# Expert dispatch sent by batch of eight token tiles instead of all at once, in a fused cross-attention and mixture-of-experts kernel

## The reference

```python
def ffn(x):                                # x: 4096 x 256, after _layernorm
    s = softmax(x @ gate_w.T); orig = s; s = s + gate_b
    # the sum of the best two in each of 4 groups picks 2 groups, then the best 2 experts of those
    idx, weights = top2(within_best_two_groups(s), values=orig)
    combine = (one_hot(idx, 16) * weights[..., None]).sum(1)
    h = silu(einsum('td,edi->tei', x, We1) + be1) * (einsum('td,edi->tei', x, We3) + be3)
    yo = einsum('tei,eid->ted', h, We2) + be2
    y = einsum('te,ted->td', combine, yo)
    z = silu(x @ ws1 + bs1) * (x @ ws3 + bs3) @ ws2 + bs2
    return y + z

x = x + align(ctx, _layernorm(x))          # dynamic time warping, its path, a scatter-add of ctx rows
x = x + ffn(_layernorm(x))
```

## Time and profile before

| | us |
|---|---|
| median of 3 runs | 546.51 (544.09 to 548.3) |
| the profiled execution's own time | 549.24 |
| its span, first to last instruction | 547.5 |
| mean granted TensorE clock | 0.806 |
| busy: PE, DVE, ACT, POOL | 309.6, 368.4, 180.0, 162.1 |
| busy share: PE, DVE, ACT, POOL | 57%, 67%, 33%, 30% |

### The profile page before, as it was taken

One profiled execution on the slowest core, in us unless ns is written; L12 is line 12 of the kernel. 1 busy time (PEld: TensorE's weight loads), 2 busy tenths in 40 slices (PEclk: granted clock), 3 DMA queues, 4 the chain that ended last, 5 costly groups with the idle time before them and its releaser, 6 DMA issues.

```text
span 547.5 us, 10073 instructions
## 1 busy us (share of the span) xinstructions
PE 309.6 (57%) x2103; PEld 220.7 (40%) x2105; DVE 368.4 (67%) x2023; ACT 180.0 (33%) x457; POOL 162.1 (30%) x186
## 2 busy tenths in 40 slices
PE   5820000000005879849883796688999998999100
PEld 4720000000002654324441562577888887878000
DVE  4869999999993696896830521635655565555297
ACT  3662000000000155651360624344665555555000
POOL 8000000000000032100777476424555555555200
PEclk9975555555556799988998799788999999999755
DMA  8305989999703000000552132133444443433499
GB/s 330 139 16 157 311 219 236 221 231 226 245 1 89 0 2 0 1 0 1 155 202 106 49 107 87 67 99 121 143 147 142 142 132 100 148 121 94 176 389 355
DMA packets 54961, 75.37 MB, mean 138 GB/s; under 512 B 11206, under 2 KB 45324, under 8 KB 53263
## 3 DMA queue, kind: packets, MB, share of 16 engines
q1 hardware_dynamic: 47983, 58.15, 37.1%
q0 software_dynamic: 6912, 16.83, 8.6%
q10 hardware_dynamic: 32, 0.02, 0.0%
HBM read 39.42 MB, written 37.64 MB: 141 GB/s over the span
## 4 chain that ended last, share of the span: by engine, by line
DVE 41%; PE 33%; another core or an unknown queue 6%; issue 6%; DMA 5%; ACT 5%; POOL 1%; DVEq 1%; SPq 0%; ACTq 0%; POOLq 0%
PE psT L854 14%; PE psT L864 6%; DVE xk L1286 5%; DVE V L1050 3%; DVE R L1018 3%; PE psD L844 3%; DVE A L1056 3%; DVE M L1024 3%; PE psT L801 2%; DVE F L1016 2%; DVE mask L1046 2%; DVE M L1014 2%; DVE A L1057 2%; PE psT L752 2%
## 5 line engine op out<-in xcount | busy, mean ns | idle before, releaser
L482 POOL DMA_INDIRECT results<-ys,idx x80 | 78.9, 986 | 79.1 <-issue 44.9
L854 PE MATMUL psT<-xsT,w_now 128*128 128x128 f32 x640 | 91.3, 287 | 6.4 <-issue 2.1
L683 PE MATMUL psT<-onesb 128*128 128x512 bf16 x24 | 9.1, 557 | 136.5 <-DVE mask L1046 136.5
L854 PEld LDWEIGHTS psT<-xsT,w_now 128*128 128x128 f32 x640 | 79.9, 196 | 15.5 <-issue 12.5
L474 POOL DMA_INDIRECT slot_rows<-stage,slot x64 | 62.8, 981 | 67.9 <-DVE slot L1208 36.1
L465 POOL TENSOR_SCALAR x2n<-xk,sm 128x256 f32<-128x256 f32 x16 | 9.0, 569 | 200.3 <-DVE sm L1082 192.9
L801 PE MATMUL psT<-x2T,sw 128*128 128x512 f32 x128 | 59.9, 618 | 12.8 <-DVE silu L1100 11.5
L683 PEld LDWEIGHTS psT<-onesb 128*128 128x128 bf16 x24 | 3.2, 136 | 141.8 <-issue 141.5
L1274 DVE SCALAR_TENSOR_TENSOR hgT<-psT,w,sg 128x128 f32<-128x128 f32 x80 | 28.1, 351 | 45.7 <-ACT sg L643 30.1
L864 PE MATMUL psT<-w,hgT 128*128 x160 | 49.8, 393 | 3.4 <-DVE hgT L1274 3.4
L634 ACT ACTIVATE w_now<-w 128x256 f32 x80 | 33.3, 417 | 44.5 <-PE psD L844 35.9
(11 more groups left out here) (180 smaller groups left out, 617.5 us busy)
## 6 DMA issues: line engine op xcount, KB each, us to landing
slot_rows<-fill SPq DMA_DIRECT2D x80, 128.5 KB, 6.6
xs<-slot_rows SPq DMA_DIRECT2D x80, 128.5 KB
xk<-in_x SPq DMA_DIRECT2D x8, 1024.0 KB, 11.0
back<-results SPq DMA_DIRECT2D x8, 1024.0 KB, 8.1
out<-xk SPq DMA_DIRECT2D x8, 512.0 KB, 8.3
w<-in_L_ffn_We SPq DMA_DIRECT2D x1, 2048.0 KB, 12.8
b<-in_L_ffn_be SPq DMA_DIRECT2D x1, 2048.0 KB
cost_skew<-zeros SPq DMA_DIRECT2D x6, 264.0 KB, 2.7
```

What stands on the lines that cost most here:

```text
L482: pool.indirect_dma_start(out=results, out_offset=bass.IndirectOffsetOnAxis(ap=idx[:, u:u + 1], axis=0), in_=ys[:, u, :], in_offset=None, ...
L854: mm = pe.matmul(psH[c % 2][:, lo:lo + P], w_now[:, c % 2, k, lo:lo + I], xsT[:, c % 2, k, :], start=(k == 0), stop=(k == KC - 1))
```

## The change

The computation is the same. Seven things differ.

1. **Rows by expert.** `slot_rows` has a fixed region of RG = 4096 + 128 rows for each expert, and 16 spare tiles at its end. A token's row is then its rank at its expert plus the region's first row, and needs no totals. The 128 rows behind each expert's last token are filled by 16 DMAs from a register once the totals are known. `rowtab` holds the first row of each loop tile, and SP reads it for every load. The loop has 79 tiles.
2. **Batches.** Choice, counting and scattering go by groups of eight tiles. After `select(g)` DVE publishes one-hots, PE's `ranks(g)` multiplies them (10 or 11 small products), DVE's `place_rows(g)` publishes `routed`, POOL sends the 16 scatters of the group. `stage` holds all 32 tiles once, with the token's number and first-choice row in two columns, and the loop tells first from second choice by comparing the row (`not_equal`).
3. **Gate by linearity.** During the alignment PE turns the raw x and multiplies it by the centred gate weights. The context's products with the gate are 16 more columns of `ctx_parts`, so `gather` yields tokens and gate sums together, 272 columns a tile, and DVE scales by the norm's factor.
4. **Order.** Adds and statistics go tile by tile (`take`), woven into the groups. Shared chunks 0 to 2 run inside groups 1 to 3, chunks 3 to 5 after them, and chunks 6 and 7 after the expert loop (EARLY = 6).
5. **Shared bias by product.** `bs2` is split in three bf16 rows, and one bf16 product with ones starts each quarter of `shared_z`. `shared_add` is one pass.
6. **Banks.** Chunks 0 and 1 put z in the banks of `psT[1]`, which half m=1 of `shared_h` uses too.
7. **Mask in four pieces** (cuts at 72, 36, 12, 0). The rows from 36 on are read back while the path is still being walked. `maskT` is copied by batch of tokens.

```diff
-SLOT_TILES = 80
+SLOT_TILES = (2 * TOK + E * (P - 1)) // P
+RG = TOK + P
+EARLY = 6
@@ SP
-            for n in range(SLOT_TILES):
-                sp.dma_start(slot_rows[n * P:(n + 1) * P, :], fill[:, :]).then_inc(filled, 16)
+            sp.wait_ge(fill_rows_ready, 1)
+            for e in range(E):
+                sp.reg_load(sp_row[e % 4], fill_row[0:1, e:e + 1])
+                at = sp.snap(sp_row[e % 4], min_val=e * RG, max_val=e * RG + TOK)
+                sp.dma_start(slot_rows[bass.ds(at, P), :], fill[:, :]).then_inc(filled, 16)
@@ POOL
             for T in range(TILES):
-                if T % HT == 0:
-                    pool.wait_ge(routed, T // HT + 1)
+                pool.wait_ge(routed, T // GT + 1)
                 pool.wait_ge(staged, T + 1)
@@ ACT
-                if T >= STAGES:
-                    act.wait_ge(scattered[T % STAGES], 32 * (T // STAGES))
@@ PE
+            def shared_h(g, m):
+                if g == 0:
+                    pe.wait_ge(maskT_ready, B)
+                    pe.wait_ge(maskT_act, B)
+                elif m == 0 or g > 2:
+                    pe.wait_ge(act_ready, 2 * g - 1 + m)
+                else:
+                    pe.wait_ge(z_used, 2 * g)
...
+            for g in range(1, TILES // GT):
+                n = GT * (g + 1)
+                more = n < TILES
+                if more:
+                    gather(n)
+                    gather(n + 1)
+                if g >= 2:
+                    shared_z(g - 2)
+                pe.wait_ge(x2T_ready, 2 * g)
+                shared_h(g - 1, 0)
+                if more:
+                    gather(n + 2)
+                    gather(n + 3)
+                turn2(4 * g)
+                turn2(4 * g + 1)
+                shared_h(g - 1, 1)
+                turn2(4 * g + 2)
+                turn2(4 * g + 3)
+                ranks(g)
+                if more:
+                    for T in range(n + 4, n + GT):
+                        gather(T)
...
+            for g in range(TILES // GT - 1, EARLY):
+                shared_h(g, 0)
+                shared_z(g - 1)
+                shared_h(g, 1)
+            shared_z(EARLY - 1)
@@ DVE
+            for g in range(TILES // GT):
...
+                take(n, n + 1)
+                dve.wait_ge(std2_ready, g + 1)
...
+                take(n + 2)
+                select(g)
+                count(g)
+                if g:
+                    weigh(g - 1)
+                if g == 0:
+                    take(n + 3)
+                if g >= 2:
+                    shared_add(g - 2)
+                place_rows(g)
+                if g:
+                    take(n + 3)
+                    shared_act(g - 1)
+                take(*range(n + 4, n + GT))
@@ DVE, in the loop
-                    dve.tensor_copy(idx[:, c % 8:c % 8 + 1], xs[:, c % 4, D:ROW]).then_inc(id_copied, 1)
+                    dve.scalar_tensor_tensor(out=idx[:, c % 8:c % 8 + 1], in0=xs[:, c % 4, D + 1:ROW],
+                                             scalar=rowf[:, bass.ds(q, 1)], in1=xs[:, c % 4, D:D + 1],
+                                             op0=ALU.not_equal, op1=ALU.add).then_inc(id_copied, 1)
```

More of the change, by code:

```diff
@@ L20 @@
 NT = CTX + QUAD - 1
+MASK_CUTS = (72, 36, 12, 0)
+MASK_HALF = 36
 TILES = B * S // P
@@ L718, in _ @@
             distances(7)
-            pe.wait_ge(const_ready, 7)
+            pe.wait_ge(gate_ready, 1)
+            for c in range(KC):
+                mm = pe.matmul(psG, mean_w[:, :], gwT[:, c, :], start=(c == 0), stop=(c == KC - 1))
+            mm.then_inc(gate_mean, 1)
+            pe.wait_ge(gate_centred, 1)
+            for b in range(B):
+                for c in range(KC):
+                    mm = pe.matmul(psQ[:, b, :], ctxT[:, c, b, :], gwT[:, c, :], start=(c == 0), stop=(c == KC - 1))
@@ L722, in _ @@
+            pe.wait_ge(xT_act, 8)
             pe.wait_ge(dist_act, 4)
             pe.wait_ge(dist_dve, 4)
-            pe.wait_ge(mask_ready, 2)
+            pe.wait_ge(x_nat, 64)
+            for n in range(8):
+                turn_nat(n)
+                if n:
+                    gate(n - 1)
+            gate(7)
+            pe.wait_ge(ctx_gate_read, 1)
+            pe.wait_ge(bs2_loaded, 16)
+            pe.wait_ge(minus_ready, 1)
+            pe.wait_ge(bs2_step, 1)
+            pe.matmul(psB, ident[:, :], bs2b[:, :], start=True, stop=False)
@@ L831, in _ @@
+            pe.wait_ge(totals_ready, 1)
+            pe.wait_ge(x2_ready, TILES)
+            pe.matmul(psN, onesb[:, :], prevb[:, TILES // GT, :], start=True, stop=True).then_inc(counted, 1)
+            pe.wait_ge(x2T_ready, TILES // 2)
+            for g in range(TILES // GT - 1, EARLY):
+                shared_h(g, 0)
                 shared_z(g - 1)
+                shared_h(g, 1)
             shared_z(EARLY - 1)
@@ new lines, in shared_add, with over_e, line @@
+            def shared_add(g):
+                for j in range(2):
+                    n = 2 * g + j
+                    dve.wait_ge(z_ready, n + 1)
+                    pair = xk[:, 2 * n:2 * n + 2, 0:D]
+                    dve.tensor_tensor(pair, z_bank(g, j).rearrange("p (t d) -> p t d", t=2), pair,
+                                      ALU.add).then_inc(z_used, 1)
+            def over_e(ap):
+                return ap.unsqueeze(2).to_broadcast([P, GT, E])
+            def line(a):
+                return a[:, :, :].rearrange("p t e -> p (t e)")
@@ L1239, in _ @@
-            dve.wait_ge(etab_ready, 1)
-            dve.wait_ge(bs2_loaded, 16)
-            for g in range(2, EARLY):
-                shared_add(g - 2)
+            start(dve.tensor_tensor(jumps[:, :, :], passed_e[:, :, :], jump[:, :].unsqueeze(1).to_broadcast(sq), ALU.mult))
+            shared_act(TILES // GT - 1)
+            link(dve.tensor_reduce(tmp[:, 0:SLOT_TILES], passed_e[:, :, :], AX.X, ALU.add))
+            dve.tensor_scalar(etab[:, :], tmp[:, 0:SLOT_TILES], float(E - 1), float(WD), ALU.min, ALU.mult)
```

776 lines of the change are left out of this document (421 added, 355 removed).

## The result

| | before | after |
|---|---|---|
| median, 4 runs each | 547.4 | 567.25 (565.29 to 568.05) |
| ratio, 95% interval | | 1.037 (1.032 to 1.042) |
| span of the profiled execution | 547.5 | 565.3 |
| first scatter | 259.1 | 205.4 |
| expert loop starts | 357.8 | 367.5 |

The forecast was 14 us faster and the result is 20 us slower, outside the range of 510 to 558. The windows of the changed kernel, by group and stage, answer to the earlier trace rows.

What follows compares the result with a forecast made beforehand. Before the loop no engine was full, but scatters and shared layer held each other up; the loop was PE's. Span 547.5 - 23.4 - 1.9 + 11.4 = 533.6, adjusted to a forecast of 533 us, range 510 to 558.

Steps and rivals of the forecast that it cites:

- rival B: PE's signals come late while POOL issues scatters, now beside the groups: 8 to 34 us lost, 541 to 567; chance 0.30.
- so at most 13 of the 34 were on the path: Scatter stage of before: PE's shared work, 85.6 of 98.7 us, hid all but 13 of 34 us of remote waits.
- Rival B in full: All 34 us of late PE signals return on the path in the groups: 567 us, slower than before; chance 0.12.
- Group times: Choice groups before the loop: slots routed at 205.8, 225.6, 261.9 and 293.1, then the loop starting at 334.4.
- The chain of half, turns and ranks: Groups 2 and 3: half m=1, two turns and ranks follow one another on PE; DVE waits 9.9 us in each.
- C: Groups run better than estimated, with shorter waits and tail gap: 10 to 20 us less, 512 to 525; chance 0.18.
- Gain before the loop: Everything ahead of the expert loop: it starts at 334.4 instead of 357.8, so -23.4 us.
- Loop: Expert loop: one tile fewer of 80 at 1.90 us each, so -1.9 us.
- Tail: After the last ys: PE computes chunks 6 and 7 there, DVE waits 7 us once, so +11.4 us.
- Mask: Mask read-back and copies ahead of the first add, put at 183.5; bounds 1.1 us earlier to 1.5 later.
- Rival D: SP's register reads in the path of the expert loop, 79 x 0.3 to 1 us: 557 to 612; chance 0.03.
- Rival E: DVE and POOL lock each other out beside groups 1 to 3: up to 46 us, half gives 556; chance 0.04.

Runs made afterwards that it cites:

- pauses of four: Changed kernel with POOL waiting for the landing after every fourth scatter: ratio 0.972 to before on one chip, 0.995 on another.
- set 3: Before, changed kernel, pauses of four, and half m=1 behind ranks with pauses of four, on one more chip: before 528.0 us; ratios 0.999, 0.994, 0.995, 0.972.
- set 2: Half m=1 behind ranks plus pauses of four (0.970), before and changed with pauses of eight (1.028, 0.995), memsets (0.994); before 527.4 us.
- memsets: Changed kernel with two small POOL memsets behind each scatter, each waited for, no wait for landings: ratio 0.994 on one chip, 0.981 on another.
- late dispatch: Changed kernel with POOL waiting for the last group's slots before its first scatter: ratio 1.094, 604 us.
- half after ranks: Changed kernel with half m=1 of each woven chunk behind the group's ranks on PE, no pauses: ratio 1.012 (558.4 us), and 1.001 on another chip.

## Why the prediction was wrong

**The step that failed** is the discount on rival B: "so at most 13 of the 34 were on the path". With it the sum had no term for held signals. Its working was wrong already: it set 85.6 us of shared work against the 98.7, where PE was busy for 71.5, and the rest is 27, not 13. For before the number came out all the same. With nothing held, the stage from the first scatter to the loop took 86.7 us (262.1 to 348.8) instead of 98.7, so 12 us were on its path, because POOL's 81 us of scatters bounded the stage anyway. But I carried the discount to the changed kernel, where it does not hold. There the chain PE, ACT, DVE, PE, DVE runs three times ahead of the next scatters and once more ahead of the loop, POOL is not the bound, and the held signals are paid nearly in full: 367.5 with them and 333.4 to 335.8 without, 32 to 34 us. Rival B in full had been priced at 34 us and 567, which is what came, and was given 0.12. That it fits to the microsecond is luck: the 34 were three of eight waits called remote in the kernel before, which sum to 63 and lie in another schedule. The rows for it stood in the earlier trace rows; I read them as costs of the old stage, not as a property of POOL's bursts that the change would place beside a longer chain.

**Group times.** Without held signals the schedule was right: slots of groups 0 to 3 at 205.8, 225.6, 261.9 and 293.1 against 205.7, 225.7, 261.6 and 290.3 (pauses of four), the loop 334.4 against 335.8. Individual sizes were off and cancelled: the half of h after idle took 5.3 us in the changed kernel, not 6.1, and the ranks were waited for 9.3 and 7.9 us instead of 9.9.

```profile
266.43 5.31 PE L908 MATMUL psT<-x2T,sw 128*128 128x512 f32 x8 [8.82 <-DVE xk L1241]
```

**The chain of half, turns and ranks** was named and is real: half m=1 behind the ranks starts the loop 9 to 14 us earlier once signals come in time (333.4 and 334.8 to 324.1 in set 3; 335.0 to 321.0 in set 2). I said under C that no product could stand in PE's gap. The half could stand behind it.

**Gain before the loop**, -23.4, was measured as -15.4 on a chip that holds nothing, since there before has no loss to give back, and as +9.7 on the chip of the result.

**Loop**, -1.9: -3.2 with held signals, -0.4 without. **Tail**, +11.4: +11.3. DVE's gap of 7 was 6.1, and it was idle time that other combines could fill. Of the 22.4 us moved, 11 were covered by these numbers, not 8 as the prediction says.

**Mask**, 183.5 for the first add: it came at 182.0, below the bound of 1.1 earlier. PE turned at 174.98 instead of 176.1 and the eight copies on DVE took 2.74. The first slots came only 0.4 us before the forecast, and nothing hangs on it.

**Rival D** had no support: PE waited 0.5 us for `xs` in the whole loop. **Rival E**: the choice step of L1289 took 0.29 us beside scatters, and 0.29 as well the two times that it ran ahead of the first one (196.71 and 198.65); the 64 scatters took 0.967 us on average, 0.98 before. In set 3, where choice steps stand beside scatters too, they follow one another every 0.33 us. Here is that step between 205 and 300 us of the changed kernel, by line on DVE: busy, mean ns, idle before.

```profile
L1289 DVE TENSOR_TENSOR t<-t,r 128x128 f32<-128x128 f32 x6 | 1.8, 292 | 0.6 <-issue 0.4
```

The lock that the Trainium skill states in "SBUF — State Buffer", section "SBUF: two separate sides", for a DVE step with two SBUF inputs is not seen in these durations. It is stated against a GpSimd step that reads SBUF, and no run here shows whether these scatters count as one.

## What to carry to other kernels

A wait that the trace ends with no instruction is a price of its own. Before moving a burst of another engine's transfers, ask who waits for signals beside it in the new place; a loss that is partly hidden under a full queue (12 us here) is paid nearly in full (32 to 34) when that queue is no longer the bound. Where indirect scatters are not the bound, issue them in groups of at most eight or with short work between. Groups of four cost nothing on the chip without the effect (0.995 against 0.994 unpaused), and on chips with it groups of four, groups of eight and memsets all started the loop some 32 us earlier than the unpaused kernel had beside the result. Where the scatters are the bound, as in the kernel before, groups of eight cost 2.8%. And measure on more than one chip: the same pair of kernels gave 1.037 and 0.994.

## What the runs showed of the hardware that I had not expected

Of five sets of runs (the result and four more), three had waits called remote in unpaused kernels, and before took 547, 552 and 547 us there. Set 3 had none, with before at 528; set 2, where before took 527, left no trace of an unpaused kernel, and only its times are like those of set 3. In the changed kernel signals of PE reached ACT and DVE 7 to 9 us late once POOL had issued indirect transfers for 13.6 us or more at 1.27 us distance, and they came 2.5 to 2.7 us after the burst. Neither number is a rule. In the kernel before a product that ended at 285.6 reached DVE at 302.40, 17 us late, but a half of h that ended at 276.9, 17.8 us into the same burst, was answered at once, as its timelines of PE and ACT show. In late dispatch two signals reached ACT 36 and 34 us late, in the middle of the burst, and one reached DVE 30 us late, 8.5 us after its end. POOL's issues were not slower (0.96 us each in both kinds).

```profile
273.28 3.60 PE L801 MATMUL psT<-x2T,sw 128*128 128x512 f32 x8
...
276.91 0.67 ACT L611 ACTIVATE silu<-psT,sb 128x512 f32<-128x512 f32 x1
...
281.95 3.62 PE L812 MATMUL psC<-sw,silu 128*128 128x256 f32 x16
```

DVE's waits for its own signals stretched too. These are DVE's choice steps of group 3 in the changed kernel, 14 to 16 us into the third burst; in set 3 the same steps follow each other every 0.33 us without an idle time. The whole choice of that group, from L1255 to L1305, took 13.9 us instead of 8.6 there. In half after ranks two of these waits are called remote themselves and took 1.75 and 2.42 us. So what is held is not only what PE sends.

```profile
289.98 0.30 DVE L1289 TENSOR_TENSOR t<-t,r 128x128 f32<-128x128 f32 x1 [0.42 <-issue]
290.67 0.29 DVE L1290 TENSOR_TENSOR t<-t,rev_e 128x128 f32<-128x128 f32 x1 [0.40 <-DVE t L1289]
291.36 0.29 DVE L1291 TENSOR_REDUCE r<-t 128x8 f32<-128x128 f32 x1 [0.40 <-DVE t L1290]
```

The expert loop, which scatters every 1.8 to 1.9 us, took 147 to 154 us in the sets with the effect and 138 to 141 in sets 2 and 3; that this is the same cause was not tested. What holds the signals, and why only some chips do it, stays open. A need to wait for landings is excluded by the memset runs, which never wait for one; that fewer transfers are on their way at a time when they are issued at 1.9 us distance is not.
